# VectorE instead of GpSimd adds the feed-forward output bias to the normalised rows, in a four-layer block on one core

## The chip, the cores and the metric

The kernel runs on one core of a Trainium2 chip. The metric is the device time of one execution in microseconds (us), lower is better; a kernel is run three times here and the median is taken.

## The reference

Four layers work on `x` (4 batches of 512 rows of 256 features), each as `x = x + layer(layernorm(x), ...)`. The change lies in the first one, an attention-free mixing layer with a feed-forward stage behind it:

```python
emb = layernorm(x) + ctx
attn = aft_local(emb, wq, bq, ..., wo, bo, pos_bias)    # exp(k), exp(w), num/den, sigmoid(q)
a = layer_norm(attn + emb, gamma, beta)
ff = relu(a @ w1 + b1) @ w2 + b2
x = x + layer_norm(ff + a, gamma, beta)
```

The row `b2` has to be added to `ff + a` before the second normalisation. Then come a mixture of 64 experts with a router (top 8), softmax attention with 16 heads, and a feed-forward stage with binarised weights.

## The kernel before

Every engine runs a program of its own, written out by hand, and the programs meet only at semaphores. All work of the first two layers' beginning stands in one function, `early_phase`, as a software pipeline over the four batches. A batch is 512 rows, held as four tiles of 128 rows by 256 features (`TT` = 4). After a prologue each engine runs the loop `for i ... for t in range(8)`. In pass `i` of it TensorE (PE) works on feed-forward tiles of batch `i` (`hidden`, `output`), on the mixing of batch `turned = i + 1`, on the first projections of batch `early = i + 2`, and, from `i` = 3 on, on the router of batch `i - 3`. The float32 products are made of high and low halves: ScalarE (ACT) copies the high half out of PSUM, VectorE (DVE) subtracts for the low half.

What one batch `b` passes through around the change, in order:

- `z_stats(b)` on DVE: adds the layer's output to the rows into `emb` (L994), takes means and variances (L906, L909).
- `root_z(b)` on GpSimd (POOL): adds epsilon and takes the power -1/2 (L573, L575, both on 128x4).
- `z_scaled(b)` on DVE: normalises `emb` in place with eight `scalar_tensor_tensor` of 128x256, four with `gamma` (L1002) and four with `beta` (L1006). The last ones raise `zn`.
- `turn_z(b)` on PE waits for `zn` and transposes `emb` (L1264); `z_high(b)` on ACT (L705) and `z_low(b)` on DVE (L1012) make the two halves; then PE's `hidden` of this batch may start.
- `add_b2(b)` on POOL (L585) waits for `zn` as well and writes `emb + b2` into `attn`, where `add_y(b)` on DVE (L845) later adds the feed-forward output. It raises `zb`, for which `emb_apply(b + 2)`, the next writer of `emb`, waits too.

POOL's own program is a single list. After the split of the first weight group it runs `root_z(0), add_b2(0), root_emb(2), add_beta(0), add_beta(1), root_z(1), add_b2(1), root_emb(3), add_beta(2), root_z(2), add_b2(2), add_beta(3)`, and then per batch `root(b, 0), root(b, 1), add_sb2(b)`, with `root_z(3), add_b2(3)` ahead of `add_sb2(0)`. `root_emb(b)` (L573, L575) gives `emb_apply(b)` on DVE (L924, four `tensor_scalar`; L927 and L929, two adds of 128x1024) its scale; `add_beta` (L591) and `add_sb2` (L597) add a row to `x_res`, each as two adds of 128x512 between two SBUF operands. DVE's `low(n)` (L824) makes the low half of a feed-forward tile from two SBUF operands.

The waits that matter for the order on POOL:

```python
def add_beta(b):
    pool.wait_ge(af["ea"], TT * b + TT)     # emb_apply(b) has read x_res
def add_sb2(b):
    pool.wait_ge(s["xn"], TT * b + TT)      # ACT has centred batch b
```

Of the kernel before, what the change touches and what calls it, by code (L numbers as in the profile page):

```python
# [19 lines left out]
ALU = mybir.AluOpType  # L20
# [8 lines left out]
TT = T // P  # L29
# [42 lines left out]
def f(ap):  # L72
    return ap.bitcast(F32)
# [326 lines left out]
def group_split(pool, g, k):  # L400

    pool.wait_ge(g.w_staged, 16 * PARTS * (k + 1))
    n = SPLITS * k
    for j, w in enumerate((g.W1, g.W2)):
        hi, lo = (w[k % 2][q][:, :, :].rearrange("p a b -> p (a b)") for q in range(2))
        for at in range(0, 2 * H, PIECE):
            cut = slice(at, at + PIECE)
            pool.tensor_copy(hi[:, cut], g.w_stage[:, j, cut]).then_inc(g.w_split, 1)
            n += 1
            pool.wait_ge(g.w_split, n)  # L410
            pool.tensor_tensor(lo[:, cut], g.w_stage[:, j, cut], f(hi[:, cut]), ALU.subtract).then_inc(g.w_split, 1)
            n += 1
# [7 lines left out]
def tiles(row, n=2):  # L420

    return row.unsqueeze(1).to_broadcast([P, n, D])
# [3 lines left out]
def early_phase(nc, g, sb, ps):  # L426
# [30 lines left out]
    emb = sb("aft_emb", [P, TT, D], F32)  # L457
# [28 lines left out]
    af = {n: sem("aft_" + n) for n in names}  # L486
# [7 lines left out]
    def attn_of(b):  # L494
        return g.attn[:, b * TT:(b + 1) * TT, :]

    def xT_of(b, q, c):
        return g.xT[q][:, c, b * T:(b + 1) * T]
# [19 lines left out]
    with nc.Block() as block:  # L518
# [41 lines left out]
        @block.gpsimd  # L560
        def _(pool):
            def root(b, k, bn, eps, rt, sh):
                pool.wait_ge(bn, TT * b + TT)
                pool.tensor_scalar(var[:, k, :], mv[:, k, :, 1], EPS, 0.0, ALU.add, ALU.add).then_inc(eps, 1)
                pool.tensor_scalar(neg[:, k, :], mv[:, k, :, 0], -1.0, 0.0, ALU.mult, ALU.add).then_inc(eps, 1)
                pool.wait_ge(eps, 2 * b + 2)
                pool.tensor_tensor(rstd[:, k, :], var[:, k, :], g.power[:, 0:TT], ALU.pow).then_inc(rt, 1)
                pool.wait_ge(rt, b + 1)
                pool.tensor_tensor(shift[:, k, :], neg[:, k, :], rstd[:, k, :], ALU.mult).then_inc(sh, 1)

            def aft_root(b, k, means, eps, done):
                pool.wait_ge(means, TT * b + TT)
                pool.tensor_scalar(var[:, k, :], mv[:, k, :, 1], EPS, 0.0, ALU.add, ALU.add).then_inc(eps, 1)  # L573
                pool.wait_ge(eps, b + 1)
                pool.tensor_tensor(rstd[:, k, :], var[:, k, :], g.power[:, 0:TT], ALU.pow).then_inc(done, 1)  # L575

            def root_emb(b):
                aft_root(b, 2, af["em"], af["ev"], af["er"])

            def root_z(b):  # L580
                aft_root(b, 3, af["zs"], af["zv"], af["zr"])

            def add_b2(b):
                pool.wait_ge(af["zn"], TT * b + TT)
                pool.tensor_tensor(attn_of(b), emb[:, :, :], tiles(g.row("b2_0"), TT), ALU.add).then_inc(af["zb"], 1)  # L585

            def add_beta(b):
                pool.wait_ge(af["ea"], TT * b + TT)
                for j in range(2):
                    part = g.x_res[:, b * TT + 2 * j:b * TT + 2 * j + 2, :]  # L590
                    pool.tensor_tensor(part, part, tiles(g.row("beta")), ALU.add).then_inc(s["beta"], 1)  # L591

            def add_sb2(b):
                pool.wait_ge(s["xn"], TT * b + TT)
                for j in range(2):
                    part = g.x_res[:, b * TT + 2 * j:b * TT + 2 * j + 2, :]
                    pool.tensor_tensor(part, part, tiles(sb2[:, :]), ALU.add).then_inc(s["sb2"], 1)  # L597

            def low_group1(j):
                w, at = (g.W1, g.W2)[j // 4], j % 4 * PIECE  # L600
                hi, lo = (w[1][q][:, :, :].rearrange("p a b -> p (a b)")[:, at:at + PIECE] for q in range(2))
                pool.wait_ge(s["g1h"], j + 1)
                pool.tensor_tensor(lo, g.w_stage[:, j // 4, at:at + PIECE], f(hi), ALU.subtract).then_inc(g.w_split, 2)

            pool.memset(g.power[:, :], -0.5).then_inc(af["pow"], 1)
            pool.wait_ge(af["pow"], 1)
            root_emb(0)
            pool.wait_ge(af["pos"], 16)
            pool.affine_select(out=pos[:, :, :], in_=pos[:, :, :], compare_op=ALU.is_ge, fill=0.0, base=BAND - 1,
                               pattern=[[-P, TT], [1, T]], channel_multiplier=-1).then_inc(af["band"], 1)  # L610
            pool.wait_ge(af["band"], 1)
            pool.affine_select(out=pos[:, :, :], in_=pos[:, :, :], compare_op=ALU.is_ge, fill=0.0, base=BAND - 1,
                               pattern=[[P, TT], [-1, T]], channel_multiplier=1).then_inc(af["band"], 1)
            root_emb(1)
            pool.tensor_tensor(sb2[:, :], g.row("sb2a"), g.row("sb2b"), ALU.add).then_inc(s["sum"], 1)
            group_split(pool, g, 0)
            root_z(0)
            add_b2(0)
            root_emb(2)
            add_beta(0)  # L620
            add_beta(1)
            root_z(1)
            add_b2(1)
            root_emb(3)
            add_beta(2)
            root_z(2)
            add_b2(2)
            add_beta(3)
            pool.wait_ge(s["sum"], 1)
            for b in range(B):  # L630
                if b == 1:
                    for j in range(4):
                        low_group1(j)
                root(b, 0, s["mv1"], s["eps1"], s["root1"], s["sh1"])
                if b == 1:
                    for j in range(4, 8):
                        low_group1(j)
                root(b, 1, s["mv2"], s["eps2"], s["root2"], s["sh2"])
                if b == 0:
                    root_z(3)  # L640
                    add_b2(3)
                add_sb2(b)
            pool.wait_ge(s["y"], FIRST)
            group_split(pool, g, 2)
# [176 lines left out]
        def _(dve):  # L821
# [135 lines left out]
            def ek_low(b):  # L957
                for j in range(2):
                    dve.wait_ge(af["ekTh"], 2 * b + j + 1)
                    dve.tensor_tensor(kT2(1, j), halves(YB[j]), f(kT2(0, j)), ALU.subtract).then_inc(af["ekTl"], 1)  # L960
# [6 lines left out]
            def den_times(b):  # L967
                for c in range(C):
                    dve.wait_ge(af["e"], 2 * b + c + 1)
                    dve.wait_ge(af["den"], 2 * b + c + 1)  # L970
                    dve.scalar_tensor_tensor(out=sg[:, c, :], in0=sg[:, c, :], scalar=1.0, in1=YB[c][:, :],
                                             op0=ALU.add, op1=ALU.mult).then_inc(af["dm"], 1)
# [26 lines left out]
            def z_scaled(b):  # L999
# [5 lines left out]
                for tt in range(TT):  # L1005
                    dve.scalar_tensor_tensor(out=emb[:, tt, :], in0=emb[:, tt, :], scalar=rstd[:, 3, tt:tt + 1],  # L1006
                                             in1=g.row("beta"), op0=ALU.mult, op1=ALU.add).then_inc(af["zn"], 1)

            def z_low(b):
                for c in range(C):  # L1010
                    dve.wait_ge(af["zth"], C * b + c + 1)
                    dve.tensor_tensor(xT_of(b, 1, c), YB[c][:, :], f(xT_of(b, 0, c)), ALU.subtract).then_inc(af["ztl"], 1)  # L1012
# [35 lines left out]
            dve.wait_ge(s["wh"], 2)  # L1048
            dve.tensor_tensor(RW[1][:, :, :], rws[:, :, :], f(RW[0][:, :, :]), ALU.subtract).then_inc(s["wl"], 1)
            dve.tensor_tensor(B2[1][:, :], b2s[:, :], f(B2[0][:, :]), ALU.subtract).then_inc(s["wl"], 1)  # L1050
            z_low(0)
            dve.wait_ge(s["wl"], 2)
            dve.sem_inc(s_pass, 1)
            for i in range(B + EARLY + 1):
                turned, early = i + 1, i + 2
                for t in range(SLOTS if i < B + EARLY else 3):
                    n = i * SLOTS + t
                    if turned < B:
                        if t == 1:
                            ek_low(turned)  # L1060
                        if t == 2:
                            den_times(turned)
                        if t == 3:
                            ekv_low(turned)
                        if t == 4:
                            make_y(turned)
                        if t == 5:
                            z_stats(turned)
                        if t == 7:
                            z_low(turned)  # L1070
                    if t == 2 and 1 <= i <= B:
                        add_y(i - 1)
# [1402 lines left out]
```

## Time and profile before

| | |
|---|---|
| median of 3 runs (lowest, highest) | 1274.57 us (1273.88, 1274.8) |
| the profiled execution: its own time | 1272.18 us |
| its span, first to last instruction | 1270.5 us |
| mean granted TensorE clock | 0.979 |
| PE busy | 1142.3 us (90%) |
| PE weight loads | 997.4 us (79%) |
| DVE busy | 878.1 us (69%) |
| ACT busy | 703.6 us (55%) |
| POOL busy | 343.7 us (27%) |

Times in rows are microseconds from the start of the span. A row of a timeline gives the start, the duration, the engine, the line, the operation, output<-inputs and the shape, how many instructions are merged in it, and in brackets how long the engine had stood idle before it and who released it.

### The profile page before, as it was taken

Reading aid. Unit: us, or ns where it says so; the run is one execution under the profiler, and the core shown is the slowest. Engines: PE = TensorE matmul, PEld = TensorE weight load, DVE = VectorE, ACT = ScalarE, POOL = GpSimd, SP = SyncE. Lnnn points to the kernel's source line nnn. Section 1 sums busy time; section 2 is a strip of 40 time slices with the busy share of each in tenths; the row PEclk is TensorE's granted clock in tenths of the full one; section 3 lists DMA queues with packets and bytes.
Section 4 is the critical chain, followed back from the end, with each engine's and each line's share of the span. In section 5 each row is a group of like instructions: output and inputs, shape, how many; then the busy total and the mean of one; then the engine's idle time right before and its main releaser. Section 6 shows DMA issues by size and latency. Waiting matters only on the chain. (4 is left out here: it accounts for less than half of the span.)

```text
span 1270.5 us, 19924 instructions
## 1 busy us (share of the span) xinstructions
PE 1142.3 (90%) x6928; PEld 997.4 (79%) x6928; DVE 878.1 (69%) x1653; ACT 703.6 (55%) x1063; POOL 343.7 (27%) x343
## 2 busy tenths in 40 slices
PE   0778899788987999999999989999999999989998
PEld 0557788677877999999999978778788788777887
DVE  3576756766674655655755443999989989997575
ACT  1213323365543444444444233888988988986755
POOL 2520202251170510600600045512442442233120
PEclk9989999899998999999999999999999999998999
DMA  9200000004334444344332023321421423310001
GB/s 313 67 1 1 1 1 1 1 1 137 71 71 112 113 115 138 94 120 134 91 95 54 1 76 100 100 58 59 136 64 54 138 62 119 95 39 5 14 24 48
DMA packets 68967, 92.88 MB, mean 73 GB/s; under 512 B 16016, under 2 KB 33168, under 8 KB 68752
## 3 DMA queue, kind: packets, MB, share of 16 engines
q1 hardware_dynamic: 67264, 89.67, 25.0%
q10 hardware_dynamic: 1616, 2.10, 0.5%
q8 instruction: 49, 0.80, 0.3%
q14 instruction: 38, 0.31, 0.1%
HBM read 80.45 MB, written 11.14 MB: 72 GB/s over the span
## 5 line engine op out<-in xcount | busy, mean ns | idle before, releaser
L1997 DVE CUSTOM_DVE_ANT_0 at_pr<-at_sc,at_mk 128x512 f32<-128x512 f32 x256 | 165.5, 683 | 26.2 <-PE at_sc L2228 25.7
L1901 ACT ACTIVATE at_pr<-at_pr,at_nmx 128x512 f32<-128x512 f32 x256 | 170.5, 717 | 17.8 <-DVE at_nmx L1997 17.2
L2139 DVE TENSOR_TENSOR W_1l<-at_pt,W_1h 128x1024 fp32r<-128x1024 f32 x128 | 155.8, 1218 | 6.1 <-ACT W_1h L1896 5.7
L1896 ACT ACTIVATE W_1h<-at_pt 128x1024 fp32r<-128x1024 f32 x128 | 130.8, 1022 | 34.7 <-PE at_o L2262 33.2
L2243 PE MATMUL at_pt<-ident,at_pr 128*128 128x128 f32 x1024 | 135.2, 275 | 15.0 <-DVE W_1l L2139 14.2
L2243 PEld LDWEIGHTS at_pt<-ident,at_pr 128*128 128x128 f32 x1024 | 115.3, 142 | 38.4 <-issue 17.0
L228 ACT ACTIVATE moe_hs<-moe_hid,cols 128x512 f32<-128x512 f32 x120 | 82.8, 690 | 100.4 <-PE moe_hid L114 99.5
L247 DVE TENSOR_TENSOR moe_hl<-moe_ms,moe_hh 128x512 fp32r<-128x512 f32 x104 | 80.4, 773 | 64.3 <-ACT moe_hh L220 64.3
L261 DVE TENSOR_TENSOR moe_ms<-moe_hs,gate 128x512 f32<-128x512 f32 x104 | 78.7, 757 | 57.4 <-ACT moe_hs L228 57.0
L220 ACT ACTIVATE moe_hh<-moe_ms 128x512 fp32r<-128x512 f32 x104 | 65.8, 633 | 94.2 <-DVE moe_ms L261 94.2
L2262 PE MATMUL at_o<-W_1h,at_vaug 128*128 128x512 f32 x256 | 112.1, 438 | 0.3 <-DVE W_1l L2139 0.3
L653 ACT ACTIVATE f_hs<-f_hid,cols 128x512 f32<-128x512 f32 x56 | 38.6, 689 | 129.2 <-PE f_hid L114 114.7
L2262 PE MATMUL at_o<-W_1l,at_vaug 128*128 128x512 f32 x256 | 101.2, 395 | 0.0
L2228 PE MATMUL at_sc<-at_kp,at_qp 128*128 128x512 f32 x256 | 82.6, 400 | 2.5 <-DVE at_nmx L1997 1.9
L114 PE MATMUL moe_y<-W_0l,moe_hh 128*128 128x256 f32 x256 | 72.4, 283 | 0.0
L114 PE MATMUL moe_y<-W_0h,moe_hl 128*128 128x256 f32 x256 | 72.4, 283 | 0.0
L114 PE MATMUL moe_y<-W_0h,moe_hh 128*128 128x256 f32 x256 | 72.1, 282 | 0.0
L824 DVE TENSOR_TENSOR f_hl<-f_hs,f_hh 128x512 fp32r<-128x512 f32 x56 | 45.0, 803 | 35.6 <-ACT f_hh L661 35.5
L1672 POOL TENSOR_TENSOR at_hs<-at_hs,at_rb 128x512 f32<-128x512 f32 x24 | 32.0, 1334 | 122.3 <-DMA at_rb<-at_recip 122.2
L114 PE MATMUL moe_y<-W_1l,moe_hh 128*128 128x256 f32 x224 | 63.4, 283 | 0.0
L114 PE MATMUL moe_y<-W_1h,moe_hl 128*128 128x256 f32 x224 | 63.4, 283 | 0.0
L114 PE MATMUL moe_y<-W_1h,moe_hh 128*128 128x256 f32 x224 | 63.1, 282 | 0.0
(304 smaller groups left out, 3304.2 us busy)
## 6 DMA issues: line engine op xcount, KB each, us to landing
gate<-expert_weights SPq DMA_DIRECT2D x256, 128.0 KB, 3.0
w_stage<-in_ew SPq DMA_DIRECT2D x32, 256.0 KB, 4.0
at_kp<-at_heads SPq DMA_DIRECT2D x96, 64.0 KB, 2.7
at_qp<-at_heads SPq DMA_DIRECT2D x96, 64.0 KB, 2.8
w_stage<-in_mask SPq DMA_DIRECT2D x16, 256.0 KB, 3.6
at_rb<-at_recip SPq DMA_DIRECT2D x64, 64.0 KB, 2.1
w_stage<-in_w SPq DMA_DIRECT2D x8, 256.0 KB, 7.3
w_stage<-in_sw SPq DMA_DIRECT2D x8, 256.0 KB, 3.3
```

What stands on the lines that cost most here:

```text
L114: last = pe.matmul(out, lhs(a, c), rhs(b, c), start=start and n == 0, stop=stop and n == m - 1, skip_group_check=skip)
L220: act.activation(m.h[0][:, prev.t % RING, :], m.ms[:, prev.t % RING, :], ACT.Copy).then_inc(m.hi_gated, 1)
L228: act.activation(m.hs[:, cur.t % 2, :], m.hid[cur.t % 2][:, :], func, bias=bias(cur), scale=1.0 if scale is None else scale(cur)).then_inc ...
L247: dve.tensor_tensor(m.h[1][:, r, :], src, f(m.h[0][:, r, :]), ALU.subtract).then_inc(m.split, 1)
L261: dve.tensor_tensor(m.ms[:, r, :], m.hs[:, cur.t % 2, :], g.gate[:, r, :], ALU.mult)\
L1896: act.activation(PH[0][:, n % 2, :], PT[n % 2][:, :, :].rearrange("p c q -> p (c q)"), ACT.Copy)\
L1901: act.activation(pr_of(t)[:, x, :], pr_of(t)[:, x, :], ACT.Exp, bias=nmx[:, t % 4, x:x + 1], scale=-1.0).then_inc(s["ex"], 1)
L1997: dve.tensor_tensor_reduce(pr_of(t)[:, x, :], SB[x][:, :], mk[u // 2 % 2][:, j, :], -float(HD) ** -0.5, 3.0e38, ALU.add, ALU.min, nmx[:, t ...
L2139: dve.tensor_tensor(PH[1][:, n % 2, :], PT[n % 2][:, :, :].rearrange("p c q -> p (c q)"), f(PH[0][:, n % 2, :]), ALU.subtract).then_inc(s[ ...
L2228: pe.matmul(SB[x][:, :], QP[:, h8, j * P:(j + 1) * P], KP[:, h8 // 2, :], start=True, stop=True)\
L2243: last = pe.transpose(PT[t % 2][:, c, j * P:(j + 1) * P], pr_of(t - i + j // 2)[:, j % 2, kc * P:(kc + 1) * P], g.ident[:, :])
L2262: last = pe.matmul(OB[:, :], w, PH[q][:, t % 2, c * T:(c + 1) * T], start=r == 0 and kc == 0 and q == 0, stop=h8 == GROUPS[k][-1] and kc = ...
```

## The change

`add_b2` moves from POOL's program to DVE's. The instruction is the same `tensor_tensor` add of 128x1024 float32. On DVE it stands directly ahead of `z_low(b)`: for batch 0 in the prologue, for the others in step `t` = 7 of the loop. On POOL nothing takes its place.

```diff
-            def add_b2(b):
-                pool.wait_ge(af["zn"], TT * b + TT)
-                pool.tensor_tensor(attn_of(b), emb[:, :, :], tiles(g.row("b2_0"), TT), ALU.add).then_inc(af["zb"], 1)
...
             root_z(0)
-            add_b2(0)
             root_emb(2)
             add_beta(0)
             add_beta(1)
             root_z(1)
-            add_b2(1)
             root_emb(3)
             add_beta(2)
             root_z(2)
-            add_b2(2)
             add_beta(3)
...
                 if b == 0:
                     root_z(3)
-                    add_b2(3)
                 add_sb2(b)
...
+            def add_b2(b):
+                dve.wait_ge(af["zn"], TT * b + TT)
+                dve.tensor_tensor(attn_of(b), emb[:, :, :], tiles(g.row("b2_0"), TT), ALU.add).then_inc(af["zb"], 1)
...
+            add_b2(0)
             z_low(0)
...
                         if t == 7:
+                            add_b2(turned)
                             z_low(turned)
```

POOL's instructions from `root_z(0)` on, as a difference of the two programs (the lines that add beta carry another number in the changed file; `aft_zn` is the semaphore that `z_scaled` raises, `aft_em` that of the statistics of `emb_stats`, `aft_ea` that of `emb_apply`):

```order
 L573 TENSOR_SCALAR rt_var<-rt_mv 128x4 [waits aft_zs]
 L575 TENSOR_TENSOR rt_rstd<-rt_var,power 128x4 [waits aft_zv]
-L585 TENSOR_TENSOR attn<-aft_emb,rows 128x1024 [waits aft_zn]
 L573 TENSOR_SCALAR rt_var<-rt_mv 128x4 [waits aft_em]
 L575 TENSOR_TENSOR rt_rstd<-rt_var,power 128x4 [waits aft_ev]
-L591 TENSOR_TENSOR x_res<-x_res,rows 128x512 [waits aft_ea]
-L591 TENSOR_TENSOR x_res<-x_res,rows 128x512
-L591 TENSOR_TENSOR x_res<-x_res,rows 128x512 [waits aft_ea]
-L591 TENSOR_TENSOR x_res<-x_res,rows 128x512
+L587 TENSOR_TENSOR x_res<-x_res,rows 128x512 [waits aft_ea]
+L587 TENSOR_TENSOR x_res<-x_res,rows 128x512
```

Between the statistics and the four adds of beta, POOL no longer has an instruction that waits for `aft_zn`.

DVE's instructions in the changed program at the end of the prologue, from `z_scaled(0)` to `emb_apply(2)`:

```order
L998 SCALAR_TENSOR_TENSOR aft_emb<-aft_emb,rt_rstd,rows 128x256 [waits aft_zg]
L998 SCALAR_TENSOR_TENSOR aft_emb<-aft_emb,rt_rstd,rows 128x256 x3
L1045 TENSOR_TENSOR rt_rwl<-rt_rws,rt_rwh 128x256 [waits fr_wh]
L1046 TENSOR_TENSOR rt_b2l<-rt_b2s,rt_b2h 128x256
L1003 TENSOR_TENSOR attn<-aft_emb,rows 128x1024 [waits aft_zn]
L1008 TENSOR_TENSOR xT_l<-rt_r,xT_h 128x512 [waits aft_zth] x2
L916 TENSOR_SCALAR aft_emb<-x_res,rt_mv,rt_rstd 128x256 [waits fr_wl,aft_zt,aft_zb,aft_ett,aft_er]
```

L1003 is the added instruction; in the program before, L1012 (here L1008) followed directly on the two small subtractions of 128x256.

## Rows read from the trace of the kernel before

**Rows 1.** The page's first part: busy time by engine.
```profile
PE 1142.3 (90%) x6928; PEld 997.4 (79%) x6928; DVE 878.1 (69%) x1653; ACT 703.6 (55%) x1063; POOL 343.7 (27%) x343
```

**Rows 2.** Timeline of PE, batch 0, end of the prologue and first pass.
```profile
88.83 1.97 PE L1264 MATMUL rt_r<-ident,aft_emb 128*128 128x128 f32 x8 [5.46 <-DVE aft_emb L1006]
...
99.56 1.09 PE L1194 MATMUL rt_r<-ident,aft_emb 128*128 128x128 f32 x8 [1.01 <-DVE aft_emb L927]
102.01 0.51 PE L114 MATMUL rt_r<-W_1h,aft_kTh 128*128 128x512 f32 x1 [1.36 <-DVE aft_kTl L960]
```

**Rows 3.** Timeline of DVE in the same stretch.
```profile
85.13 0.38 DVE L909 BATCH_NORM_AGGREGATE rt_mv<-rt_st 128x2 f32<-128x6 f32 x4
...
87.10 1.67 DVE L1006 SCALAR_TENSOR_TENSOR aft_emb<-aft_emb,rt_rstd,rows 128x256 f32<-128x256 f32 x4
...
91.46 0.69 DVE L1012 TENSOR_TENSOR xT_l<-rt_r,xT_h 128x512 fp32r<-128x512 f32 x1 [0.16 <-ACT xT_h L705]
93.01 5.23 DVE L924 TENSOR_SCALAR aft_emb<-x_res,rt_mv,rt_rstd 128x256 f32<-128x256 f32 x4 [0.86 <-POOL rt_rstd L575]
```

**Rows 4.** Timeline of POOL in the same stretch.
```profile
84.21 1.03 POOL L575 TENSOR_TENSOR rt_rstd<-rt_var,power 128x4 f32<-128x4 f32 x1
...
92.95 5.14 POOL L591 TENSOR_TENSOR x_res<-x_res,rows 128x512 f32<-128x512 f32 x4
```

**Rows 5.** The moved instruction on POOL, and DVE's add of one shape: ns min/median/max.
```profile
L585 POOL TENSOR_TENSOR attn<-aft_emb,rows x4: 2369/2391/2802, 88.9 to 250.9; 128x1024 f32<-128x1024 f32 x4
...
L929 DVE TENSOR_TENSOR attn<-aft_emb,rows x4: 1224/1225/2167, 18.2 to 155.5; 128x1024 f32<-128x1024 f32 x4
```

**Rows 6.** Timeline of DVE: emb_apply of batch 0, POOL idle.
```profile
15.57 1.38 DVE L924 TENSOR_SCALAR aft_emb<-x_res,rt_mv,rt_rstd 128x256 f32<-128x256 f32 x4 [6.06 <-DMA rows<-in_rows]
```

**Rows 7.** Timeline of POOL, batch 2, pass 1.
```profile
194.32 1.03 POOL L575 TENSOR_TENSOR rt_rstd<-rt_var,power 128x4 f32<-128x4 f32 x1
...
202.29 2.55 POOL L591 TENSOR_TENSOR x_res<-x_res,rows 128x512 f32<-128x512 f32 x2
```

**Rows 8.** Timeline of DVE in the same stretch.
```profile
195.87 0.69 DVE L824 TENSOR_TENSOR f_hl<-f_hs,f_hh 128x512 fp32r<-128x512 f32 x1 [1.73 <-ACT f_hh L661]
...
203.67 1.72 DVE L824 TENSOR_TENSOR f_hl<-f_hs,f_hh 128x512 fp32r<-128x512 f32 x1 [1.15 <-ACT f_hh L661]
```

**Rows 9.** Timeline of PE in the same stretch.
```profile
199.91 1.09 PE L1264 MATMUL rt_r<-ident,aft_emb 128*128 128x128 f32 x8 [1.17 <-DVE aft_emb L1006]
...
205.45 0.39 PE L114 MATMUL f_y<-W_0h,f_hh 128*128 128x256 f32 x1 [0.25 <-DVE f_hl L824]
```

**Rows 10.** Timeline, batch 3, pass 2: POOL.
```profile
253.23 2.54 POOL L597 TENSOR_TENSOR x_res<-x_res,rt_sb 128x512 f32<-128x512 f32 x2
```

**Rows 11.** Timeline, batch 3, pass 2: ACT.
```profile
246.71 2.06 ACT L717 ACTIVATE rt_xn<-x_res,rt_shift,rt_rstd 128x256 f32<-128x256 f32 x4
```

**Rows 12.** Timeline, batch 3, pass 2: DVE.
```profile
249.15 1.67 DVE L1006 SCALAR_TENSOR_TENSOR aft_emb<-aft_emb,rt_rstd,rows 128x256 f32<-128x256 f32 x4
...
253.52 0.69 DVE L1012 TENSOR_TENSOR xT_l<-rt_r,xT_h 128x512 fp32r<-128x512 f32 x1 [0.16 <-ACT xT_h L705]
```

**Rows 13.** Timeline, batch 3, pass 2: PE.
```profile
250.88 1.97 PE L1264 MATMUL rt_r<-ident,aft_emb 128*128 128x128 f32 x8 [3.62 <-DVE aft_emb L1006]
```

**Rows 14.** Timeline of DVE, batch 1, pass 0.
```profile
140.96 1.67 DVE L1006 SCALAR_TENSOR_TENSOR aft_emb<-aft_emb,rt_rstd,rows 128x256 f32<-128x256 f32 x4
144.01 1.29 DVE L1012 TENSOR_TENSOR xT_l<-rt_r,xT_h 128x512 fp32r<-128x512 f32 x2 [1.38 <-ACT xT_h L705]
```

**Rows 15.** Timelines of POOL and of DVE: a small power and an add of two SBUF operands.
```profile
304.97 1.03 POOL L567 TENSOR_TENSOR rt_rstd<-rt_var,power 128x4 f32<-128x4 f32 x1
...
305.48 0.69 DVE L831 TENSOR_TENSOR f_hs<-f_hs,gate 128x512 f32<-128x512 f32 x1 [1.19 <-ACT f_hs L653]
```

**Rows 16.** PE, batch 1; and a window there: busy by engine, granted clock, DMA.
```profile
155.49 1.97 PE L1194 MATMUL rt_r<-ident,aft_emb 128*128 128x128 f32 x8 [3.82 <-DVE aft_emb L927]
...
155.40:158.60 3.20, 3.11 (x15) 3.11 (x16) 3.17 (x6) 1.20 (x2) 0.00 (x0) 0.50 0.00 0
```

## The prediction, made before the run

> **What bounds the kernel now.** I read the busy times first: PE is busy for 1142.3 us, 90% of the span, POOL for 27% [rows 1]. So what counts is where PE stands idle, and whether the moved instruction, or what follows it on POOL and on DVE, sits in front of such an idle stretch. Next I read PE's timeline around the four places. For every batch PE waits for the last instruction of `z_scaled` (L1006) before it transposes `emb`: 5.46 us for batch 0 [rows 2], 1.17 us for batch 2 [rows 9], 3.62 us for batch 3 [rows 13]. PE works through one list, so whatever delays `z_scaled` there delays all behind it by the same amount. Then I read POOL and DVE in these stretches, for what each does at the same moment.
>
> **The instruction itself.** POOL needs 2.39 us (2.80 once) for the add of 128x1024, DVE 1.22 us for an add of the same shape, also from two SBUF operands [rows 5]. Four of them are 4 x 1.22 = 4.9 us more on DVE. They stand between the end of `z_scaled` and `z_low`. For batch 1, `z_scaled` ends at 142.63 and `z_low` starts at 144.01, after an idle time of 1.38 us [rows 14]: 1.22 us fits. For batch 0, `z_low` could first start at 91.46 - 0.16 - 0.69 = 90.61, which is 1.84 us after 88.77, the end of `z_scaled` [rows 3]; the two small subtractions (about 0.35 us each by their size, an estimate from rows 3) and the add take 1.9 us. Nothing in sum. The cover is the way over PE and ACT; without it each add would cost its 1.22 us.
>
> **What it frees on POOL.** `add_b2` waited for the end of `z_scaled`, and held back what stands behind it on POOL. Without it, POOL's next adds start earlier, and this is the real change.
>
> *Do POOL's adds and DVE disturb each other?* Yes, where DVE reads two SBUF operands or runs its fast one-input form. `low` (L824) took 1.72 us at 203.67, in the midst of POOL's two adds of beta that ran from 202.29 [rows 7], and 0.69 us at 195.87, with POOL idle [rows 8]: it waited until the second add ended at 204.84 and then ran. The four L924 of `emb_apply` took 1.38 us with POOL idle [rows 6] and 5.23 us beside four adds of POOL (5.14 us), one of them per add [rows 3, 4]. `z_low` (L1012), with one operand in PSUM, kept its 0.69 us at 253.52 beside POOL's adds from 253.23 [rows 10, 12]. `z_scaled` (L1002, L1006) has two SBUF operands like L824, but no row shows it beside an add of POOL; I take it to wait, as L824, its nearest row, does.
>
> The Trainium skill says as much in "SBUF — State Buffer", section "SBUF: two separate sides": VectorE and GpSimd share a port pair, which a GpSimd instruction or a VectorE instruction with two SBUF inputs holds for its whole length. And "Perfetto Trace Analysis", section "Optimizing Scalar/DVE Operations", warns that moving work between these two might not help, for this reason.
>
> *Batch 0.* The statistics for `root_emb(2)` are there at 85.51 [rows 3]. The power takes 1.03 us [rows 4], the small operation ahead of it some 0.4 us, so the four adds of beta start at about 87.0 instead of 92.95, just when the four L1006 start (87.10). One L1006 then goes by per add. The pitch is at least that of L924, 5.23 / 4 = 1.31 us; at most add and L1006 one behind the other, 5.14 / 4 + 1.67 / 4 = 1.70 us. I take 1.40, since L1006 alone is hardly longer than L924 alone (0.42 against 0.35 us), the row that it is nearest to. End of `z_scaled`: 87.0 + 4 x 1.40 + 0.2 = 92.8 instead of 88.77, 4.0 us later (bounds 3.5 and 5.0). PE, ACT and `z_low` follow. Behind that something comes back: `emb_apply(2)` now finds POOL idle and its scale ready, and takes 1.38 instead of 5.23 us, so PE's later waits of 1.01 us for it and 1.36 us for `ek_low` [rows 2] go. What is late next is PE's own work. Net 4.0 - 1.0 - 1.4 = 1.6 us, rather 1.5 as the transposes overlap their neighbours (bounds 1.0 and 2.6).
>
> *Batch 1.* POOL's next instruction, `root_emb(3)`, waits for statistics that DVE makes after `z_low`; nothing moves. 0.
>
> *Batch 2.* The power of `root_z(2)` ends at 195.35 [rows 7] and `add_beta(3)` now runs there, not at 202.29. `low` at 195.87 [rows 8] waits for the first add, 0.7 us; the first L1002 behind it waits for the second add, 1.1 us. `z_scaled` ends 1.8 us later (1.3 to 2.3), and PE's 1.17 us wait grows by that [rows 9]. The disturbed `low` at 203.67 is free again, worth what PE waited for it, 0.25 us, say 0.3.
>
> *Batch 3.* `add_sb2(0)` waits for ACT, which is done at 248.77 [rows 11]; it now runs there, not at 253.23 [rows 10]. Two of the L1006 from 249.15 [rows 12] wait for one add each: 249.1 + 2 x 1.4 + 2 x 0.42 = 252.8 against 250.82, so 2.0 us (1.6 to 2.5), all of it PE's wait [rows 13].
>
> **Sum:** 1.5 + 0 + 1.8 - 0.3 + 2.0 = 5.0 us, with bounds of 3.6 and 7.1. The profiled execution took 1272.18 us, which gives 1277.2; the median of the runs shown lies 2.4 us above it, so 1274.57 + 5.0 = 1279.6. A measurement of this kernel can tell about 0.2%, 2.5 us, from no change.
>
> **A row against a rule.** POOL's power of 1.03 us at 304.97 did not disturb the multiplication of two SBUF operands at 305.48, which took 0.69 us [rows 15]. So I let `root_emb(2)` cost `z_scaled(0)` nothing. The Trainium skill's rule (same page and section) has any GpSimd instruction hold the port from start to end. As a mechanism of this kernel that is a rival of its own: the L1002 that is due at about 86 waits for most of the 1.03 us power, and the sum is 6.0 us, 1280.6. Chance 0.07, since the only row speaks against it.
>
> **The rivals.**
> *`z_scaled` does not wait* (chance 0.18). Two tensor inputs and a scalar from a pointer is another instruction than L824's. Then in batch 0 only the two small subtractions and the new add wait, one POOL add each, behind the second, third and fourth: 92.1 + 1.2 = 93.3, `z_low` ends at 94.6 instead of 92.15, +2.4 us, and the same 2.4 us come back. Batch 2 costs 0.7 - 0.3 us, batch 3 nothing. +0.4 us, 1275.0: no change. Against it: the operands are placed as L824's are.
>
> *Faster: POOL yields* (chance 0.08). POOL's first `add_b2` took 2.80 instead of 2.39 us, beside the two small subtractions of DVE [rows 5]; so DVE can make POOL wait. If POOL's beta adds fit themselves between DVE's instructions in batch 0, `z_low(0)` ends at 92.15 as before, `emb_apply(2)` starts 0.9 us sooner and lasts 3.85 us less, and PE's two waits go: -2.4 - 0.3 = -2.7 us, 1271.9. It decides this way only while `z_scaled(0)` stays under 2.4 us of delay. Against it: beside four adds, the four L924 lost 3.85 us and the adds nothing.
>
> *The clock* (chance 0.17). Behind a wait of 3.82 us PE was granted 0.50 of its clock, 1.2 of 2.4 GHz, for 3.2 us, and lost half of that, 1.6 us [rows 16]. The wait for batch 2 grows to 3.0 us. If that is enough there, or the longer waits for batches 0 and 3 lengthen their slow stretches, the sum grows by 1.6 to 3.2 us: 1281.2 to 1282.8.
>
> **How the numbers follow.** Forecast 0.50, the power holding 0.07, clock 0.17, `z_scaled` free 0.18, POOL yields 0.08. The likeliest is 1279.6. The range takes in the forecast's bounds (1278.2 to 1281.7), the clock and the free `z_scaled`: 1274.4 to 1282.7. Slower by over 0.2%: 0.50 + 0.07 + 0.17, less 0.03 for delays that are taken up further on, 0.71. Within 0.2%: 0.18 + 0.03 and the weaker half of the faster rival, 0.23. Faster: 0.06.
>
> **What the profile of the changed kernel would show.** Right: the L1006 of batch 0 take some 5.5 us for four instead of 1.67, beside beta adds from about 87.0; L924 of batch 2 takes 1.38 us; `low` near 196 takes 1.3 us or more; L1006 of batch 3 some 3.7 us; PE's waits for L1006 are 9.5, 3.0 and 5.6 us. Wrong: L1006 stays at 1.67 us with POOL's adds beside it (`z_scaled` free), or the adds are stretched instead (POOL yields); `z_low` of batch 1 starting later than 1.4 us after `z_scaled` would make the added instruction itself a cost.

## The result, and the profile after

The changed kernel took 1282.57 us (median of 4 runs, 1281.61 to 1283.63), the kernel before 1274.51 us (median of 4). The ratio is 1.0065, with a 95% interval of 1.0046 to 1.0085: slower by 8 us. The forecast was 1279.6 us, with a range up to 1282.7; 1.0065 times the 1274.57 us it started from is 1282.9 us, just above. An execution that took far longer than the others of its kernel is left out of the medians and ratios below. The direction came out as forecast, and so did the mechanism behind the longer waits; the size was too small, because the forecast had no term for TensorE's clock.

The first part of the page of the changed kernel, with the columns of [rows 1]:

```profile
span 1280.6 us, 19924 instructions
PE 1147.5 (90%) x6928; PEld 1001.6 (78%) x6928; DVE 885.9 (69%) x1657; ACT 703.8 (55%) x1063; POOL 334.7 (26%) x339
```

DVE is busy for 7.8 us more, POOL for 9.0 us less; of DVE's, 4 x 1.23 us are the moved instruction, most of the rest is waiting inside instructions. PE is busy for 5.2 us more with the same 6928 products: that is, for the most part, what the forecast left out.

**The mechanism.** POOL's timeline of the changed kernel at batch 0, then DVE's, against [rows 4] and [rows 3]. In the changed file all lines behind the moved function carry other numbers: the first four of `z_scaled` are L994 (L1002 before), the last four L998 (L1006), the moved add L1003, `z_low` L1008 (L1012), `low` L816 (L824), `emb_apply`'s `tensor_scalar` L916 (L924), the adds of beta L587 (L591).

```profile
86.13 1.11 POOL L575 TENSOR_TENSOR rt_rstd<-rt_var,power 128x4 f32<-128x4 f32 x1
87.21 5.46 POOL L587 TENSOR_TENSOR x_res<-x_res,rows 128x512 f32<-128x512 f32 x4
```
```profile
85.50 1.64 DVE L994 SCALAR_TENSOR_TENSOR aft_emb<-aft_emb,rt_mv,rows 128x256 f32<-128x256 f32 x4
87.17 5.78 DVE L998 SCALAR_TENSOR_TENSOR aft_emb<-aft_emb,rt_rstd,rows 128x256 f32<-128x256 f32 x4
...
93.55 1.21 DVE L1003 TENSOR_TENSOR attn<-aft_emb,rows 128x1024 f32<-128x1024 f32 x1
94.79 0.69 DVE L1008 TENSOR_TENSOR xT_l<-rt_r,xT_h 128x512 fp32r<-128x512 f32 x1
...
96.25 1.37 DVE L916 TENSOR_SCALAR aft_emb<-x_res,rt_mv,rt_rstd 128x256 f32<-128x256 f32 x4
```

The four adds of beta start at 87.21 instead of 92.95, and the last four instructions of `z_scaled` take 5.78 us instead of 1.67: one per add, as the four `tensor_scalar` of `emb_apply(2)` did before. Those now take 1.37 us instead of 5.23. The power of 1.11 us did not disturb L994, which took 1.64 us beside it, as in the kernel before. The moved instruction (L1003) costs its 1.21 us in the shadow of PE's transposes.

DVE at batch 2 and at batch 3 of the changed kernel:

```profile
200.15 1.30 DVE L816 TENSOR_TENSOR f_hl<-f_hs,f_hh 128x512 fp32r<-128x512 f32 x1 [1.73 <-ACT f_hh L653]
201.38 2.71 DVE L994 SCALAR_TENSOR_TENSOR aft_emb<-aft_emb,rt_mv,rows 128x256 f32<-128x256 f32 x4
...
256.17 3.56 DVE L998 SCALAR_TENSOR_TENSOR aft_emb<-aft_emb,rt_rstd,rows 128x256 f32<-128x256 f32 x4
```

`low` is 0.61 us longer than the 0.69 us of [rows 8] and the first four of `z_scaled` 1.04 us longer than the 1.67 us that they took before; at batch 3 the last four are 1.89 us longer than in [rows 12]. PE's side, against [rows 2, 9, 13]:

```profile
93.01 1.97 PE L1262 MATMUL rt_r<-ident,aft_emb 128*128 128x128 f32 x8 [9.59 <-DVE aft_emb L998]
...
205.85 1.28 PE L1262 MATMUL rt_r<-ident,aft_emb 128*128 128x128 f32 x8 [2.82 <-DVE aft_emb L998]
...
259.78 1.97 PE L1262 MATMUL rt_r<-ident,aft_emb 128*128 128x128 f32 x8 [5.51 <-DVE aft_emb L998]
```

**Where the rest is.** I paired PE's products of the two traces and took the difference of their starts. The first product of the denominators of batch 1 starts 1.0 us later (103.03 against 102.01): the transposes in front of it had started 4.18 us later (93.01 against 88.83), and the rest was won back. The transposes of batch 2 start 5.9 us later and those of batch 3 8.9 us, the last product ends 10.1 us later. Of the 10.1 us, 1.0 + 1.65 - 0.34 + 1.89 = 4.2 us are the waits for `z_scaled`, net of what comes back at batch 0 and, 0.34 us, at batch 2. The other 5.9 us come while PE works, product by product, where the changed kernel runs at half clock and the kernel before at full clock: 1.6 us from 121 us on, 1.6 from 179, 1.5 from 206, 0.6 from 257, and 0.6 in sum behind that. The two profiled executions lie further apart than the medians, since that of the kernel before was 2.3 us under its median (1272.18 against 1274.51); between the medians, 8.1 us apart, about 3.9 us are left for the clock. Windows of the kernel before, and then of the changed kernel (busy PE with its products, PEld, DVE, ACT, POOL; granted clock; DMA share, GB/s):

```profile
87.07:97.31 10.24, 6.98 (x24) 5.83 (x25) 8.02 (x12) 2.85 (x5) 8.38 (x7) 0.50 0.01 2
119.10:122.50 3.40, 3.40 (x15) 2.83 (x16) 3.22 (x2) 0.14 (x1) 0.00 (x0) 1.00 0.01 2
177.00:180.40 3.40, 3.40 (x16) 2.79 (x16) 3.40 (x2) 0.00 (x0) 0.00 (x0) 1.00 0.02 5
199.90:203.30 3.40, 3.39 (x24) 3.13 (x25) 1.29 (x2) 1.96 (x4) 3.37 (x2) 1.00 0.02 5
250.91:254.32 3.41, 3.41 (x12) 3.06 (x13) 1.38 (x2) 1.20 (x2) 3.41 (x2) 0.50 0.02 5
```
```profile
87.15:100.80 13.65, 6.29 (x23) 5.23 (x23) 12.71 (x15) 2.36 (x4) 5.52 (x5) 0.50 0.00 1
121.28:124.69 3.41, 3.41 (x9) 2.62 (x8) 3.06 (x2) 0.00 (x0) 0.00 (x0) 0.50 0.01 2
179.31:182.72 3.41, 3.41 (x10) 2.65 (x9) 3.41 (x2) 0.00 (x0) 0.00 (x0) 0.50 0.02 5
206.61:210.03 3.42, 3.42 (x13) 2.83 (x11) 1.76 (x3) 1.43 (x3) 0.00 (x0) 0.50 0.02 5
257.81:264.64 6.83, 4.86 (x17) 4.28 (x18) 4.53 (x6) 1.49 (x3) 0.85 (x1) 0.50 0.01 2
```

The changed kernel has three stretches at half clock (0.50, 1.2 GHz), each of about 3.4 us, where the kernel before runs at full clock: at 121, 179 and 206. In the first two PE did 9 and 10 products of 128x512 in the time of 15 and 16. In front of each of these two stands a wait for `ekv_low` (L957) that the kernel before has too (L965), at the same length, 2.1 us. This is the first of them, in the kernel before and then in the changed kernel:

```profile
119.03 0.50 PE L114 MATMUL rt_r<-W_1h,aft_kTh 128*128 128x512 f32 x1 [2.09 <-DVE aft_kTl L965]
```
```profile
120.03 0.50 PE L114 MATMUL rt_r<-W_1h,aft_kTh 128*128 128x512 f32 x1 [2.09 <-DVE aft_kTl L957]
```

The third, at 206, stands right behind the wait that grew from 1.17 to 2.82 us. The stretch of batch 0 grew from 10.24 to 13.65 us and cost nothing: PE did 6.29 us of work in it instead of 6.98.

### The profile page after: what moved, and what is told of

Read it like the earlier page. It is cut to its first block and busy times, and to the rows that moved or that the text cites. A ratio compares the mean times of both kernels' runs of the same rounds, so it can differ in the third digit from the quotient of the medians.

```text
span 1280.6 us, 19924 instructions
## 1 busy us (share of the span) xinstructions
PE 1147.5 (90%) x6928; PEld 1001.6 (78%) x6928; DVE 885.9 (69%) x1657; ACT 703.8 (55%) x1063; POOL 334.7 (26%) x339
## 5 line engine op out<-in xcount | busy, mean ns | idle before, releaser
L816 DVE TENSOR_TENSOR f_hl<-f_hs,f_hh 128x512 fp32r<-128x512 f32 x56 | 44.5, 795 | 40.3 <-ACT f_hh L653 40.1
```

## The experiments

Two questions were left. Is it the early start of POOL's adds that costs, or the instruction given to DVE? And is the second half of the loss the clock? Each run is compared with the kernel before on the same chip. The ratios count, as the median of the kernel before was between 1274.35 and 1276.93 us there.

**POOL waits where its add stood.**

```diff
             root_z(0)
+            pool.wait_ge(af["zn"], TT)
             root_emb(2)
```
and in the same way behind `root_z(1)`, `root_z(2)` and `root_z(3)` of the changed kernel.

> The changed kernel, but POOL waits for the end of z_scaled (zn) at the four places where its add of b2 stood; DVE still makes that add. Port theory (POOL's beta and sb2 adds, started too early, stall z_scaled): the four L998 of each batch take 1.67 us again and PE's four waits for them sum to about 11.4 us instead of 19.1; the time falls back to 1272 to 1276 us. Rival (the added instruction on DVE is the cost): z_scaled and the waits may change, but the time stays within 2 us of 1282.6.

Measured: 1272.05 us, ratio 0.9982 (0.9967 to 0.9998). PE's waits, first as changed, then with this edit (us in total, times, longest):

```profile
PE rt_r L1262 <- DVE aft_emb L998: 19.1, 4, 9.6
```
```profile
PE rt_r L1266 <- DVE aft_emb L1002: 11.4, 4, 5.5
```

With the added instruction still on DVE, the whole loss is gone, and the half-clock stretches near 121, 179 and 206 with it. The instruction is not the cost.

**POOL's order alone.** In the kernel before, nothing goes to DVE; on POOL `add_b2` of batches 0, 2 and 3 stands behind the adds that it held back.

```diff
             root_z(0)
-            add_b2(0)
             root_emb(2)
             add_beta(0)
             add_beta(1)
+            add_b2(0)
...
             root_z(2)
-            add_b2(2)
             add_beta(3)
+            add_b2(2)
```
(and `add_b2(3)` behind `add_sb2(0)`)

> The kernel before, with add_b2 of batches 0, 2 and 3 still on POOL but behind the adds of beta and sb2 that it used to hold back; DVE gets nothing. Port theory: z_scaled of batch 0 takes 5.8 instead of 1.67 us for its last four, PE's waits for it sum to about 19 us, and the time is 1279 to 1284 us, without any work moved to DVE. Rival (the added instruction on DVE is the cost): 1273 to 1276 us.

Measured: 1283.42 us, ratio 1.0059 (1.004 to 1.0078), PE's waits for `z_scaled` 19.1 us. Two rows of POOL's timeline and DVE's at batch 0:

```profile
87.52 5.46 POOL L591 TENSOR_TENSOR x_res<-x_res,rows 128x512 f32<-128x512 f32 x4
93.34 2.46 POOL L585 TENSOR_TENSOR attn<-aft_emb,rows 128x1024 f32<-128x1024 f32 x1 [0.36 <-DVE aft_emb L1007]
```
```profile
87.48 5.78 DVE L1007 SCALAR_TENSOR_TENSOR aft_emb<-aft_emb,rt_rstd,rows 128x256 f32<-128x256 f32 x4
...
93.52 2.57 DVE L1051 TENSOR_TENSOR rt_b2l<-rt_b2s,rt_b2h 128x256 fp32r<-128x256 f32 x1
```

This makes the whole loss without moving any work to DVE. Together the two runs settle the first question: what the change costs comes from POOL running its adds beside `z_scaled` and, at batch 2, the `low` ahead of it.

**Which batch.** Two partial holds of the changed kernel. In the first, POOL waits for `zn` of batch 0 ahead of `add_beta(0)`:

> The changed kernel with one wait more: POOL starts its beta adds of batches 0 and 1 only when z_scaled(0) has ended; its early adds in batches 2 and 3 stay. Port theory: PE's wait for L1006 of batch 0 is 5.5 us again, those of batches 2 and 3 stay at 2.8 and 5.5 us; in waiting that leaves 1.7 + 1.8 us against the kernel before, less 1 to 2 us for the earlier root_emb(2), and something for the clock: 1276 to 1280 us. If batch 0 were the whole of it: 1274.5 us or less.

Measured: 1277.72 us, ratio 1.0012 (0.999 to 1.0033), PE's waits for `z_scaled` 15.0 us. In the second it waits ahead of `add_beta(3)` and of `add_sb2(0)` only:

> The changed kernel, with POOL's beta add of batch 3 and sb2 add of batch 0 held until z_scaled of their batch has ended; batch 0 stays as changed. Port theory: PE's waits for z_scaled sum to 15.5 us (9.6, 0.4 for batch 1, 1.2, 3.7 and what else there was), batch 0 keeps its net 1.0 us plus clock: ratio to the kernel before 1.001 to 1.005. If batches 2 and 3 did nothing it would stay at 1.0065.

Measured: 1276.63 us, ratio 1.0011 (0.9994 to 1.0028), waits 15.5 us. So the waits add up: 11.4 + 3.6 + 4.1 = 19.1 us. The times don't tell how the loss splits: neither half can be told from no change while both together cost 0.5 to 0.65%, and the upper ends of the two intervals would still allow an even split. The traces tell more. With batch 0 held, the half-clock stretches stand there all the same, a little earlier:

```profile
118.38:121.79 3.41, 3.41 (x10) 2.63 (x9) 3.06 (x2) 0.00 (x0) 0.00 (x0) 0.50 0.01 2
176.41:179.82 3.41, 3.41 (x10) 2.67 (x9) 3.41 (x2) 0.00 (x0) 0.00 (x0) 0.50 0.02 5
```

The second run has them too, at 121.17 and 179.19, but not the one near 206, whose wait is back at 1.17 us. In the first run nothing is late yet at 118 us: PE's wait for `ekv_low` ends there at 117.11, 1.9 us earlier than in the kernel before. So the first of these stretches does not need the longer wait of batch 0, and it comes before anything that batches 2 and 3 do. The profiled execution of the first run took 1280.11 us, near the upper end of its run (1273.72 to 1280.53); the shorter ones had a higher mean clock (0.976 at 1273.72 us against 0.972).

**The change once more**, since the kernel before spread over 1269 to 1280 us in other runs:

> The changed kernel, unaltered, once more beside the kernel before: the earlier runs of the kernel before spread from 1269 to 1280 us. If the 8 us are the change's own, the ratio is again 1.004 to 1.008, with PE's waits for z_scaled at 19.1 us; if they were luck of the clock, it comes under 1.003.

Measured: 1283.17 us, ratio 1.0051 (1.0033 to 1.0068), waits 19.1 us. The loss is the change's own. Two of its ten executions took 1277.6 and 1277.8 us, at a mean granted clock of 0.975 and 0.976, the other eight 1281.1 to 1284.7 us at 0.970 to 0.972: some 5 us can come and go by the clock with the program unchanged.

**Holding the adds where they hurt nobody.** The changed kernel, with

```diff
             root_emb(2)
+            pool.wait_ge(af["ab"], 3)
             add_beta(0)
...
             root_emb(3)
+            pool.wait_ge(af["ab"], 4)
             add_beta(2)
```
and `zn` of batches 2 and 3 ahead of `add_beta(3)` and `add_sb2(0)`. `ab` at 3 (4) tells that `emb_apply` of batch 2 (3) is through.

> The changed kernel, with POOL's beta adds of batches 0 to 2 held until emb_apply of the later batch has ended, and its beta add of batch 3 and sb2 add of batch 0 held until z_scaled of that batch has ended; root_emb(2) stays early. Port theory: z_scaled takes 1.67 us, the four tensor_scalar of emb_apply take 1.4 us for batches 2 and 3 alike (3.29 us for batch 3 before), PE's wait for emb_apply(3) falls from 3.8 to about 1.9 us; against the kernel before that is 2.4 + 1.9 us less waiting, so 1268 to 1272 us, with up to 3 us either way for the clock. Rival (DVE's add is the cost): above 1277 us.

Measured: 1269.91 us, ratio 0.9967 (0.9949 to 0.9985). The kernel before with the two `ab` waits alone:

> The kernel before, b2 still added by POOL, with the beta adds of batches 0 to 2 held until emb_apply of the later batch has ended. Port theory: the tensor_scalar of emb_apply(2) take 1.4 instead of 5.23 us and those of emb_apply(3) 1.4 instead of 3.29 us; PE waits 2.3 + 1.9 us less; 1269 to 1273 us. If the port did not matter it would be 1274.5.

Measured: 1269.13 us, ratio 0.9957 (0.9935 to 0.9979). DVE in the first of the two, and PE's wait for `emb_apply`, which was 3.82 us in [rows 16]:

```profile
92.07 1.38 DVE L920 TENSOR_SCALAR aft_emb<-x_res,rt_mv,rt_rstd 128x256 f32<-128x256 f32 x4
...
148.49 1.38 DVE L920 TENSOR_SCALAR aft_emb<-x_res,rt_mv,rt_rstd 128x256 f32<-128x256 f32 x4 [0.92 <-POOL rt_rstd L575]
```
```profile
PE rt_r L1196 <- DVE aft_emb L923: 1.9, 1, 1.9
```

Both are faster than the kernel before, and their intervals overlap: once POOL's adds stay away from `z_scaled` and `emb_apply`, it makes no difference that can be measured which engine adds `b2`.

**The clock.** Products that nobody reads keep PE at work in front of its wait for `z_scaled`. They leave no computation out.

```diff
             def turn_z(b):
+                pe.wait_ge(af["z"], 2 * b + 2)
+                for _ in range((24, 4, 4, 15)[b]):
+                    pe.matmul(YB[0][:, :], W[0][:, 0, 0, 0:P], ewT[0][:, 0, :], start=True, stop=True)
                 pe.wait_ge(af["zn"], TT * b + TT)
```

> The kernel before, with matrix products that no one reads put on PE in front of each wait for z_scaled (24, 4, 4 and 15 of 128x512 for batches 0 to 3), into a PSUM bank that is free then; they keep PE at work while it would wait. Clock theory: the stretches at a granted clock of 0.5 near 87 and 251 us go, the span falls by 1 to 4 us. If the clock were of no consequence: unchanged, or longer by what the products delay.

Measured: 1277.34 us, ratio 1.0001 (0.9983 to 1.0018). The stretches near 87 and 251 were gone, but the time did not fall: with its batch-0 work done sooner, PE then waited 4.08 us for `emb_apply(2)`, still slowed by POOL, and ran at half clock behind that. The expected gain did not come; this is a miss. At batch 0 a gain of clock in front of a fixed wait was only waited for; later on this run had a half-clock stretch at 178.67 that the kernel before does not have.

> The changed kernel with the same products (42, 4, 11 and 23, since its waits are longer). Clock theory: of the 8 us between the two kernels 4.5 are waits for z_scaled net of what comes back, the rest is clock; with PE kept at work the difference to the kernel before with fill is 2.5 to 5 us, and the stretches at half clock near 121, 179 and 207 us are gone. Rival (the whole difference is waiting): it stays at 8 us.

Measured: 1274.01 us, ratio 0.999 (0.9974 to 1.0005). Windows of the filled kernel before, and then of the filled changed kernel:

```profile
88.00:98.00 10.00, 5.30 (x30) 3.86 (x28) 7.68 (x10) 3.95 (x7) 9.15 (x7) 1.00 0.00 0
98.00:107.00 9.00, 6.57 (x21) 5.18 (x22) 5.23 (x7) 1.09 (x2) 0.00 (x0) 0.62 0.00 0
```
```profile
88.00:101.00 13.00, 11.00 (x59) 8.89 (x58) 12.93 (x17) 3.13 (x6) 5.27 (x4) 1.00 0.00 0
118.97:122.38 3.41, 3.41 (x9) 2.65 (x8) 3.41 (x2) 0.00 (x0) 0.00 (x0) 0.50 0.01 2
178.00:182.00 4.00, 4.00 (x19) 3.30 (x18) 3.96 (x3) 0.00 (x0) 0.00 (x0) 1.00 0.00 0
202.00:206.00 4.00, 3.70 (x25) 3.03 (x24) 3.22 (x5) 1.82 (x4) 0.00 (x0) 1.00 0.00 0
```

POOL's adds slowed `z_scaled` as much as in the changed kernel (its last four took 5.93 us at batch 0), yet the loss is gone: the half-clock stretches at 179 and 206 are absent, the one near 120 is not. I had expected the filled changed kernel to be 2.5 to 5 us behind the filled kernel before; it came out 3.3 us ahead, with overlapping ratios. That is a miss as well. The two have different numbers of products put in, and the filled kernel before had half-clock stretches of its own. So this run shows that the clock can carry the whole loss away, and not how large its part in the change is; for that there are only the paired products above.

**Both together.** The kernel before, with the held adds and the fill:

> The kernel before with the gated beta adds of e4_before_gated and the fill of f1_before_fill. Both act on different stretches, so the gains add: 1264 to 1269 us. If the fill gives nothing: 1269 us.

Measured: 1267.0 us, ratio 0.9931 (0.9909 to 0.9953). The changed kernel with its own held adds and the same fill:

> e3_gated (b2 added by DVE, POOL's adds held) with the products of f1_before_fill. If the side on which b2 is added is worth nothing once POOL's adds are held, it lands within 2 us of h1_gated_fill, at 1265 to 1270 us, ratio about 0.993; if DVE's added instruction costs, it is 3 us or more above it.

Measured: 1266.0 us, ratio 0.9912 (0.988 to 0.9943). Both beat both kernels, and cannot be told apart. By the middles the fill is worth more here than in the kernel before; that this is because `emb_apply(2)` no longer holds PE back is not shown.

## What the prediction had right, and the step that failed

- **The instruction itself, nothing in sum:** right. L1003 took 1.21 to 1.23 us four times, and the run with POOL's waits put back lost nothing.
- **Batch 0, 4.0 us at `z_scaled`, net 1.5:** right. 9.59 - 5.46 = 4.1 us, net 1.0 us; the pitch of 1.40 was 5.78 / 4 = 1.45 us. The choice of L824 as the nearest row, because both read two SBUF operands, was what decided. No row had shown `z_scaled` beside an add; it was taken from its nearest row, and held.
- **Batch 1, nothing:** right, `z_low` starts at 146.62, 1.38 us behind the end of `z_scaled` at 145.24, as before.
- **Batch 2, 1.8 us and batch 3, 2.0 us:** right; 1.65 and 1.89 us. The 0.3 us given back at batch 2 came too: the starts of PE's products in the two traces drew together by 0.34 us there.
- **The small power holds nobody:** right, L994 kept 1.64 us beside it. The rival of a free `z_scaled` and the one of a yielding POOL are out: POOL's adds took 5.46 instead of 5.14 us, DVE's last four 5.78 instead of 1.67.
- **The clock:** this is where it failed. Net, the waits make 4.2 us against the 5.0 of the sum, and 5.9 us more between the two traces are clock, for which the sum had no term. The clock stood only in a rival with a chance of 0.17: "The wait for batch 2 grows to 3.0 us. If that is enough there, or the longer waits for batches 0 and 3 lengthen their slow stretches, the sum grows by 1.6 to 3.2 us". It priced the clock only where a wait grows. All three of its stretches came; in the paired starts they cost 1.5 us at 206.61, 0.6 us at 257.81 to 264.64 and nothing at 87.15 to 100.80. Beside them came half-clock stretches at 121 and 179, behind waits that had not grown; their worth, 3.3 us between 102 and 199 us in the paired starts, was in no term. The range, too, took the clock on top of the middle of the forecast (1279.6 + 3.2) and not on top of its upper bound.

What stays open is why those two begin where they do. The same 2.1 us wait stands ahead of them in both kernels. It does not take a longer time slow or idle at batch 0: with batch 0 held, PE's waits there were 5.44, 1.50 and 0.22 us, against 5.46, 1.50, 1.01 and 1.36 us in the kernel before, its half-clock stretch was of the same 10.24 us, and the stretch at 118.38 came all the same. What differs is when the wait falls. It ended at 117.11 us in that run and at 116.98 us in the run with all of POOL's waits put back, which stayed at full clock; no run moves the wait alone. How much clock such a change costs was therefore in part luck.

## What to carry to other kernels

When an instruction leaves a queue, look at what it was holding back there, and at what that will run beside: here the moved add cost nothing, and freed adds of GpSimd next to two-operand instructions of VectorE (four beside four at batch 0, two beside two at batches 2 and 3) cost everything. Two to four lines of waiting that keep such adds away from this work and from the `tensor_scalar` of `emb_apply` were worth 0.3 to 0.4%, while the choice of engine for `b2` was then worth nothing measurable. And where TensorE waits for some microseconds several times in a row, as here, a change of a few microseconds can bring as much again in clock, or not; a range for such a kernel has to hold that.

## What the hardware showed that I had not expected

- A short instruction of DVE can last as long as one of POOL's: the subtraction of 128x256, 0.41 us in the changed kernel with POOL idle, took 2.57 us beside POOL's add of 128x1024 in the run with POOL's order alone. It goes the other way too. This is POOL's small operation on 128x4, which takes 0.23 us alone, in the run in which POOL waits for `zn`; its time covers one of DVE's small subtractions and its add of 128x1024:

```profile
87.97 1.81 POOL L573 TENSOR_SCALAR rt_var<-rt_mv 128x4 f32<-128x4 f32 x1 [3.62 <-DVE aft_emb L1002]
```

- What the two engines lose to each other is lopsided: in the changed kernel, four POOL adds beside four DVE instructions took 5.46 us, 0.3 us longer than in the kernel before and 0.4 us longer than the 5.02 us of the run with held adds; the four DVE instructions took 4.1 us longer. POOL in the run with held adds:

```profile
96.04 5.02 POOL L587 TENSOR_TENSOR x_res<-x_res,rows 128x512 f32<-128x512 f32 x4 [8.88 <-DVE attn L925]
```

The Trainium skill's "SBUF — State Buffer", section "SBUF: two separate sides", has the loser wait for the whole instruction of the other; the trace agrees for adds of 128x512, and not for the power on 128x4, beside which DVE lost nothing.

- The granted clock of PE fell to 0.50 (1.2 GHz) at 121.28 in the changed kernel, 1.2 us after PE had begun to work again behind a wait of 2.1 us, in the middle of a dense run of products. The kernel before had the same wait and stayed at 1.00, so it was not the idle time just before alone that decided.
